# Expert and output projections of part 2: one fp32 product of unsplit operands where three products of fp16 halves stood

## The reference

```python
rw = _gating(hidden_states, sim_matrix, gates)          # (b, t, 16), softmax over the active experts
q = jnp.einsum('bte,bted->btd', rw, jnp.einsum('btc,ecd->bted', hidden_states, q_proj))
k = jnp.einsum('bte,bted->btd', rw, jnp.einsum('btc,ecd->bted', hidden_states, k_proj))
v = jnp.einsum('bte,bted->btd', rw, jnp.einsum('btc,ecd->bted', hidden_states, v_proj))
scores = jnp.einsum('bqd,bkd->bqk', q, k) * scale       # scale = 1/8, causal
attn = jnp.einsum('bqk,bkd->bqd', jax.nn.softmax(scores, axis=-1), v)
mixed = attn[:, :, None, :] * rw[..., None]
return jnp.einsum('bted,edc->btc', mixed, o_proj)
```

## Time and profile before

| what | value |
|---|---|
| median of 3 timed runs | 1654.61 us (1653.49 to 1655.23) |
| profiled execution, from first to last instruction | 1653.4 us |
| PE busy | 1530.0 us (93%) |
| DVE busy | 1406.8 us (85%) |
| ACT busy | 1156.5 us (70%) |
| POOL busy | 1032.0 us (62%) |
| L743 MATMUL (experts) | x1536, 143.8 us busy |
| L783 MATMUL (y) | x768, 48.8 us busy |
| mean granted TensorE clock | 0.977 |

### The profile page before, as it was taken

One profiled execution on the slowest core, in us unless ns is written; L12 is line 12 of the kernel. 1 busy time (PEld: TensorE's weight loads), 2 busy tenths in 40 slices (PEclk: granted clock), 3 DMA queues, 4 the chain that ended last, 5 costly groups with the idle time before them and its releaser, 6 DMA issues. The chain is left out here.

```text
span 1653.4 us, 28187 instructions
## 1 busy us (share of the span) xinstructions
PE 1530.0 (93%) x8882; PEld 844.4 (51%) x8882; DVE 1406.8 (85%) x2161; ACT 1156.5 (70%) x2191; POOL 1032.0 (62%) x715
## 2 busy tenths in 40 slices
PE   3699999999999999999999999999983599999997
PEld 1344444444434444444444444444432599998997
DVE  5999999989999999999999899999997466656665
ACT  3888887788878877777788787787763355545553
POOL 3777777777777777777777677777773433323330
PEclk8999999999999999999999999999996799999999
DMA  4221111111211111111111111111002000000000
GB/s 110 68 62 44 43 27 44 27 46 37 54 26 43 30 38 43 26 43 37 51 32 43 26 43 43 26 26 26 1 1 52 1 6 8 8 9 8 7 9 10
DMA packets 51462, 53.00 MB, mean 32 GB/s; under 512 B 17057, under 2 KB 32929, under 8 KB 51361
## 3 DMA queue, kind: packets, MB, share of 16 engines
q1 hardware_dynamic: 51360, 51.76, 12.3%
HBM read 7.68 MB, written 2.10 MB: 6 GB/s over the span
## 5 line engine op out<-in xcount | busy, mean ns | idle before, releaser
L472 POOL TENSOR_TENSOR prob<-prob 128x1024 f32<-128x1024 f32 x256 | 603.7, 2358 | 252.1 <-DVE prob L1264 251.9
L911 ACT ACTIVATE prob<-score_ps,negmax 128x1024 f32<-128x1024 f32 x512 | 571.2, 1116 | 170.0 <-DVE negmax L1223 158.5
L1223 DVE TENSOR_REDUCE negmax<-score_ps 128x1 f32<-128x1024 f32 x512 | 620.1, 1211 | 64.2 <-PE score_ps L576 62.8
L605 PE MATMUL attn_ps<-probT,v_sb 128*64 128x512 f32 x1024 | 536.2, 618 | 0.8 <-ACT attnT L928 0.8
L576 PE MATMUL score_ps<-ka,qa 128*128 128x512 f16 x1024 | 311.8, 387 | 34.3 <-ACT prob L911 22.8
L840 ACT ACTIVATE probT<-trans_ps 128x512 f32<-128x512 f32 x480 | 285.4, 595 | 6.9 <-PE trans_ps L599 6.9
L599 PE MATMUL trans_ps<-ident,prob 128*128 128x128 f32 x2048 | 269.6, 274 | 2.5 <-POOL prob L472 2.5
L599 PEld LDWEIGHTS trans_ps<-ident,prob 128*128 128x128 f32 x2048 | 240.0, 141 | 56.4 <-POOL prob L472 3.9
L524 POOL TENSOR_TENSOR xs<-xnT,rw_all 128x2048 f32 (+1 forms) x32 | 115.5, 3611 | 210.1 <-PE t_ps L729 203.4
L576 PEld LDWEIGHTS score_ps<-ka,qa 128*128 128x128 f16 x1024 | 69.6, 98 | 341.1 <-ACT prob L911 274.4
L468 POOL TENSOR_TENSOR prob<-prob,ccol 128x384 f32<-128x384 f32 x256 | 211.6, 827 | 49.9 <-DVE ccol L1236 31.1
(11 more groups left out here) (196 smaller groups left out, 1425.4 us busy)
## 6 DMA issues: line engine op xcount, KB each, us to landing
qa<-split SPq DMA_DIRECT2D x256, 64.0 KB, 2.0
ka<-split SPq DMA_DIRECT2D x256, 64.0 KB, 2.0
xg<-xnT SPq DMA_DIRECT2D x16, 512.0 KB, 3.0
resid<-in_L_attn_x SPq DMA_DIRECT2D x4, 512.0 KB, 5.9
wg<-in_L_attn_Wkv SPq DMA_DIRECT2D x32, 64.0 KB, 1.9
out<-yo SPq DMA_DIRECT2D x32, 64.0 KB, 1.5
wg<-in_L_attn_Wq SPq DMA_DIRECT2D x16, 64.0 KB, 1.9
ew<-in_L_ffn_q_proj SPq DMA_DIRECT2D x1, 512.0 KB, 4.4
```

The lines of the kernel that those rows point to most:

```text
L472: pool.tensor_tensor(prob1[:, u, :], prob1[:, u, :], prob2[:, u, :], ALU.add).then_inc(mix_ok, 1)
L605: return pe.matmul(attn_ps[head * DV:(head + 1) * DV, :], v_sb[:, (half // 2) % 2, kt, head * DV:(head + 1) * DV], probT[:, half % 2, kt, ...
L911: act.activation(prob2[:, s % 4, :] if sub else prob1[:, s % 4, :], score_ps[:, sub, :], ACT.Exp, bias=negmax[:, s % 2, sub:sub + 1], accu ...
L1223: dve.tensor_reduce(negmax[:, s % 2, sub:sub + 1], score_ps[:, sub, :], AX.X, ALU.max, negate=True).then_inc(max_ok, 1)
```

## The change

The operands of both projections stay fp32 and are not split. `experts` issues one fp32 product for each expert (16 a tile, 128x128 by 128x192), y one for each pair of experts (8 a tile). The fp16 halves of the weights, their scale of 64, and with them four ACT passes and two POOL passes before part 2, are gone. Each bank of `t_ps` is now read once, as fp32, bank 0 by ACT and bank 1 by DVE, in place of ACT and then DVE for each bank. So a bank's next use, and the product that reads the group, wait for one engine (`xT_A` or `xT_V`, `mT_A` or `mT_V`) where they waited for the second of two.

```diff
--- before.py
+++ after.py
@@ -509,10 +506,6 @@
...
             pool.wait_ge(resid_ok, 2 * STEPS)
-
-            for n, (w, split_w) in enumerate(((ew, ew_split), (eow, eow_split))):
-                pool.wait_ge(w_hi, n + 1)
-                pool.tensor_tensor(split_w[:, 1, :, :], w[:, :, :], split_w[:, 0, :, :], ALU.subtract).then_inc(w_lo, 1)
             pool.wait_ge(g_nP, 2)
@@ -691,7 +684,7 @@
...
             gate_logits(B - 1)
-            pe.wait_ge(w_lo, 2)
+            pe.wait_ge(experts_in, 16 * 5)
             pe.wait_ge(rw_ok, 1)
@@ -706,18 +699,18 @@
-                        pT = (pT_A, pT_V)[bank]
+                        xT, pT, mT = ((xT_A, pT_A, mT_A), (xT_V, pT_V, mT_V))[bank]
                         for what in before:
                             if what == "x0" and live(0):
-                                return pe.wait_ge(xT_lo, 4 * m + bank + 1)
+                                return pe.wait_ge(xT, 2 * m + 1)
                             if what == "x1" and live(0):
-                                return pe.wait_ge(xT_lo, 4 * m + 2 + bank + 1)
+                                return pe.wait_ge(xT, 2 * m + 2)
                             if what == "x1 of m - 1" and live(1):
-                                return pe.wait_ge(xT_lo, 4 * (m - 1) + 2 + bank + 1)
+                                return pe.wait_ge(xT, 2 * m)
                             if what == "p" and live(2):
...
                             if what == "y of m - 1" and live(4):
-                                return pe.wait_ge(mT_lo, 2 * (m - 4) + bank + 1)
+                                return pe.wait_ge(mT, m - 3)
@@ -733,15 +726,13 @@
...
                             return
-                        pe.wait_ge(xT_lo, 4 * m + group + 1)
+                        pe.wait_ge((xT_A, xT_V)[group % 2], 2 * m + group // 2 + 1)
                         if group == 0 and not (first and t == 0):
...
                         for e in range(4 * group, 4 * group + 4):
-                            for n, (x_part, w_part) in enumerate(SPLIT_PRODUCTS):
-                                mm = pe.matmul(qkv_ps[:, 0:3 * DE], xsT[:, t % 2, x_part, e, :], ew_split[:, w_part, e, :],
-                                               start=e == 0 and n == 0, stop=e == E - 1 and n == 2)
+                            mm = pe.matmul(qkv_ps[:, 0:3 * DE], xsT[:, t % 2, e, :], ew[:, e, :], start=e == 0, stop=e == E - 1)
                         if group == 3:
@@ -775,13 +766,12 @@
...
                     if live(4):
-                        pe.wait_ge(mT_lo, 2 * (m - 3))
+                        pe.wait_ge(mT_A, m - 3)
+                        pe.wait_ge(mT_V, m - 3)
                         if not (first and t == 4):
...
                         for g in range(8):
-                            for n, (x_part, w_part) in enumerate(SPLIT_PRODUCTS):
-                                mm = pe.matmul(y_ps[:, 0:C], mxT[:, x_part, g, :], eow_split[:, w_part, g, :],
-                                               start=g == 0 and n == 0, stop=g == 7 and n == 2)
+                            mm = pe.matmul(y_ps[:, 0:C], mxT[:, g, :], eow[:, g, :], start=g == 0, stop=g == 7)
                         mm.then_inc(y_ok, 1)
@@ -972,12 +962,6 @@
-            act.wait_ge(experts_in, 16 * 5)
-            for w in (ew, eow):
-                act.activation(w[:, :, :], w[:, :, :], ACT.Copy, scale=WSCALE).then_inc(w_scaled, 1)
-            for n, (w, split_w) in enumerate(((ew, ew_split), (eow, eow_split))):
-                act.wait_ge(w_scaled, n + 1)
-                act.activation(split_w[:, 0, :, :], w[:, :, :], ACT.Copy).then_inc(w_hi, 1)
             act.wait_ge(g_v, GEXP)
@@ -994,11 +978,10 @@
...
                             act.wait_ge(qkv_ok, m - 1)
-                        act.activation(xsT[:, t % 2, 0, 4 * group:4 * group + 4, :],
-                                       t_ps[:, group % 2, :].rearrange("p (e q) -> p e q", e=4), ACT.Copy).then_inc(xT_hi, 1)
+                        act.activation(xsT[:, t % 2, 4 * group:4 * group + 4, :],
+                                       t_ps[:, 0, :].rearrange("p (e q) -> p e q", e=4), ACT.Copy).then_inc(xT_A, 1)
                     x_copy(0)
-                    x_copy(1)
                     if live(1):
@@ -1026,12 +1008,10 @@
...
                     if live(3):
-                        for bank in range(2):
-                            act.wait_ge(mT_ps, 2 * (m - 3) + bank + 1)
-                            if bank == 0 and not (first and t == 3):
-                                act.wait_ge(y_ok, m - 3)
-                            act.activation(mxT[:, 0, 4 * bank:4 * bank + 4, :],
-                                           t_ps[:, bank, :].rearrange("p (g q) -> p g q", g=4), ACT.Copy).then_inc(mT_hi, 1)
+                        act.wait_ge(mT_ps, 2 * (m - 3) + 1)
+                        if not (first and t == 3):
+                            act.wait_ge(y_ok, m - 3)
+                        act.activation(mxT[:, 0:4, :], t_ps[:, 0, :].rearrange("p (g q) -> p g q", g=4), ACT.Copy).then_inc(mT_A, 1)
                     if live(0):
@@ -1379,19 +1359,19 @@
...
                             return
-                        dve.wait_ge(xT_hi, 4 * m + group + 1)
-                        dve.tensor_tensor(xsT[:, t % 2, 1, 4 * group:4 * group + 4, :],
-                                          t_ps[:, group % 2, :].rearrange("p (e q) -> p e q", e=4),
-                                          xsT[:, t % 2, 0, 4 * group:4 * group + 4, :], ALU.subtract).then_inc(xT_lo, 1)
-
-                    x_copy(0)
+                        dve.wait_ge(xT_ps, 4 * m + group + 1)
+                        if group == 1 and not (first and t < 2):
+                            dve.wait_ge(qkv_ok, m - 1)
+                        dve.tensor_copy(xsT[:, t % 2, 4 * group:4 * group + 4, :],
+                                        t_ps[:, 1, :].rearrange("p (e q) -> p e q", e=4)).then_inc(xT_V, 1)
@@ -1422,19 +1401,18 @@
...
                     if live(3):
-                        for bank in range(2):
-                            dve.wait_ge(mT_hi, 2 * (m - 3) + bank + 1)
-                            dve.tensor_tensor(mxT[:, 1, 4 * bank:4 * bank + 4, :],
-                                              t_ps[:, bank, :].rearrange("p (g q) -> p g q", g=4),
-                                              mxT[:, 0, 4 * bank:4 * bank + 4, :], ALU.subtract).then_inc(mT_lo, 1)
+                        dve.wait_ge(mT_ps, 2 * (m - 2))
+                        if not (first and t == 3):
+                            dve.wait_ge(y_ok, m - 3)
+                        dve.tensor_copy(mxT[:, 4:8, :], t_ps[:, 1, :].rearrange("p (g q) -> p g q", g=4)).then_inc(mT_V, 1)
```

More of the change, by code:

```diff
@@ L87 @@
 GATE_LEAST = 1e-12
-WSCALE = 64.0
 PART2_LAG = 4
@@ L230, in block_kernel @@
         xs = sb("xs", [P, 2, E, C])
-        ew_split = sb("ew_split", [P, 2, E, 3 * DE], F16)
-        eow_split = sb("eow_split", [P, 2, E // 2, C], F16)
-        xsT = sb("xsT", [P, 2, 2, E, P], F16)
+        xsT = sb("xsT", [P, 2, E, P])
         kv2 = sb("kv2", [P, NT, 2 * DE])
@@ L243, in block_kernel @@
         mx = sb("mx", [P, 2, E, DE])
-        mxT = sb("mxT", [P, 2, E // 2, P], F16)
+        mxT = sb("mxT", [P, E // 2, P])
         yo = sb("yo", [P, 2, C])
@@ L274, in block_kernel @@
         const2_in, iota_ok, mask_ok = sem("const2_in"), sem("iota_ok"), sem("mask_ok")
-        g_top, w_scaled, w_hi, w_lo = sem("g_top"), sem("w_scaled"), sem("w_hi"), sem("w_lo")
+        g_top = sem("g_top")
         c2_v, c2_a, c2_p = sem("c2_v"), sem("c2_a"), sem("c2_p")
@@ L279, in block_kernel @@
                                     "normed_V", "T", "A", "V", "lg", "v", "exp", "rw"))
-        (xs_ok, xT_ps, xT_hi, xT_lo, qkv_ok, hi2, lo2, kv_read, kv_first_ok, qkt_ps, qkt_ok, s2_ok, max2, exp2, pT_ps,
-         pT_A, pT_V, pv2, rec2_ok, mx_ok, mT_ps, mT_hi, mT_lo, y_ok, y_done) = (sem("p2_" + n) for n in (
-            "xs", "xT_ps", "xT_hi", "xT_lo", "qkv", "hi", "lo", "kv_read", "kv_first", "qkt_ps", "qkt", "s", "max", "exp",
-            "pT_ps", "pT_A", "pT_V", "pv", "rec", "mx", "mT_ps", "mT_hi", "mT_lo", "y", "y_done"))
+        (xs_ok, xT_ps, xT_A, xT_V, qkv_ok, hi2, lo2, kv_read, kv_first_ok, qkt_ps, qkt_ok, s2_ok, max2, exp2, pT_ps,
+         pT_A, pT_V, pv2, rec2_ok, mx_ok, mT_ps, mT_A, mT_V, y_ok, y_done) = (sem("p2_" + n) for n in (
+            "xs", "xT_ps", "xT_A", "xT_V", "qkv", "hi", "lo", "kv_read", "kv_first", "qkt_ps", "qkt", "s", "max", "exp",
+            "pT_ps", "pT_A", "pT_V", "pv", "rec", "mx", "mT_ps", "mT_A", "mT_V", "y", "y_done"))
         stored = [sem("stored0"), sem("stored1")]
@@ L1044, in tiles2 @@
                             act.wait_ge(qkt_ps, m - 1)
-                        act.activation(qs[:, t % 2, 0, 0:DE], qkv_ps[:, 0:DE], ACT.Copy, scale=DE ** -0.5 / WSCALE).then_inc(hi2, 1)
```

(9 more changed lines are left out.)

4 lines of the change are left out of this document (removed).

## The result

| | before | after |
|---|---|---|
| median of the runs | 1654.92 us (1653.49 to 1655.72, 4 runs) | 1687.36 us (1686.29 to 1689.16, 4 runs) |
| ratio, 95% interval | | 1.0199 [1.0185, 1.0214] |
| profiled span | 1653.4 us | 1684.5 us |
| part 2 starts (first transpose of xs) | 1292.8 | 1288.4 |
| length of part 2 | 360.6 | 396.1 |

A forecast was written before the change was run, and what follows sets the result against it. PE was taken to bound part 2: 54.9 - 10.8 - 4.4 - 1.9 - 3.1 = 34.7 us on the span of 1653.4 gives 1688.1, and a median of 1689.3 us; range 1682 to 1703.

The forecast's parts named there:

- The added products: PE in part 2: fp32 products add 40.7 us in the experts and 14.2 in y, plus 54.9 us.
- Both ends of the range (112 and 214 ns): Bounds for a 192-column fp32 record on PE: experts 12.0 us less than before, or 92 more; 163.5 ns was taken.
- The transposes of mx: PE's waits before and inside these transposes in part 2 shrink from 12.4 to 1.6 us, a gain of 10.8.
- First tiles and tail: PE's waits for bank copies shrink where part 2's pipeline is not filled (4.4 us) and in the last turns (1.9).
- the third of the forecast's three places: One of three places in the first tiles where experts wait behind x transposes; together they gain 2.1 us.
- The gate: On the path to rw_all, L1350 and L1351 on DVE run free of POOL's weight splits: 3.1 us less.
- The stall of PE at the turn of part 2's loop: PE's stall at the loop's turn comes from no data and stays, so no gain was counted.
- The rival of the weight loads: Five groups of fp32 products a turn each pay 0.10 us more: 16 us added, 1705; chance 0.07.
- DVE's copies are not held up by POOL: Rival judged: DVE's copies in part 2 wait until POOL's xs ends, 3.8 us a turn, 1811; chance 0.03.
- That the waits stay: Rival: PE's waits move elsewhere, for example to a late ACT; 10.8 us are not gained, 1700; chance 0.07.
- The faster case: Rival: a 192-column fp32 record costs 112 ns like one of 128, so the kernel takes 1637; chance 0.02.

The follow-up runs named there:

- c64: The changed kernel with 64 columns in place of 192 in the products of the 14 inner experts; 1642.91 us in one run.
- relief_only: The kernel before with each bank read once, three fp16 products kept, xs and mx not split; 1636.46 us, ratio 0.9897.
- work_only: The kernel before with the unsplit fp32 products, each bank still read by ACT and then by DVE; 1704.64 us, ratio 1.0305.
- before_unrolled: The kernel before with PE's loop over batches 1 and 2 in part 2 written out; 1649.05 us, ratio 0.9969.
- after_unrolled: The changed kernel with PE's loop over batches 1 and 2 in part 2 written out; 1687.39 us, ratio to before 1.0197.
- p_first: The changed kernel with the transposes of the probabilities ahead of experts(0); 1686.04 us in one run.

## Why the prediction was right, and where it was not

**The added products** (forecast 54.9). 1024 x 0.1625 = 166.4 for 126.7, and 512 x 0.1117 = 57.2 for 43.0: 39.7 + 14.2 = 53.9. Taking the record's time as twice its columns at 2.4 GHz, from the 512-column row, was right; 163.5 was 1.0 ns too much, for the reason that c64 shows. Both ends of the range (112 and 214 ns) were far off, and the choice between them carried the forecast.

**The transposes of mx** (forecast -10.8). 12.3 us became 1.3: -11.0. relief_only and work_only show that the handover does it and the products do not. (One time on the way was summed wrongly: DVE's copy of bank 1 ends 1.08 + 0.69 = 1.77 us behind the start of the x transposes, not 1.83, and 1.76 in after.)

**First tiles and tail** (forecast -4.4 and -1.9). From x transposes to experts 3.2 became 1.0; the third of the forecast's three places, where experts(2) follows the values product, went from 0.9 to 0.2; from q and k to experts(0) 1.4 became 0.2: -4.2. The three last turns went from 5.6 to 3.6: -2.0, with waits of 1.31, 1.31 and 0.99 (forecast 1.4, 1.4 and 1.0).

**The gate** (forecast -3.1). -3.1 by its rows, and part 2 starts 4.4 us sooner. The other 1.3 are part 1, which the change leaves alone and which varies: in the profiles here part 2 starts anywhere from 1288.4 to 1294.6.

**The step that failed**: "The stall of PE at the turn of part 2's loop comes from no data and stays." It comes from no data, that was read rightly, but code is also something that a change changes. It went: 3.0 us, and 1.5 at the lower clock behind it, -4.5 in all. before_unrolled (part 2 is 4.6 us shorter) and after_unrolled (0) show that these were the loop's.

**The step that was missing**: 3.5 us inside the experts' groups, at the two places where an fp32 record follows a 16-bit product of 56 ns. The rival of the weight loads named the likely mechanism, with 0.10 us at five places a turn; it is 0.056 at two. Its 0.10 came from a row that c64's reading does not explain, since it lies behind a record of 512 columns. p_first shows one of the two places by an edit; the other is read from its row alone (1487.64 to 1489.00, 1.36 us for eight).

Together in part 2: 53.9 - 11.0 - 4.2 - 2.0 - 4.5 + 3.5 = 35.7, measured 35.5; less the 4.4 of the earlier start 31.1, which is the difference of the spans, where 34.7 were forecast. Of the 3.6 too much, 1.0 are the failed and the missing step (opposite in sign, -4.5 and +3.5), 1.3 part 1, 1.0 the record's price, and a few tenths lie in the small terms. The medians differ by 32.4, since after's median lies 2.9 above its profiled span and before's 1.5. That the failed and the missing step nearly cancel was luck, and the time came closer than the steps deserved.

**The other rivals.** DVE's copies are not held up by POOL: the 96 of part 2 have means of 687 and 682 ns, against the 675 and 691 of the earlier trace rows, though POOL's xs runs beside many of them. The groups over the whole kernel:

```profile
L1365 DVE COPY xsT<-t_ps 128x512 f32<-128x512 f32 x64 | 44.0, 687 | 55.0 <-PE t_ps L722 54.8
L1407 DVE COPY mxT<-t_ps 128x512 f32<-128x512 f32 x32 | 21.8, 682 | 0.6 <-PE t_ps L762 0.6
```

The lock of the shared port pair, which the Trainium skill tells of (SBUF — State Buffer, section SBUF: two separate sides), does not show on a copy out of PSUM here, while L1350 and L1351 of the gate did run 1.22 and 1.86 us longer beside POOL's splits; without POOL's splits these two take 0.19 and 0.69. The trace agrees with the rule for those two, whose inputs lie in SBUF; the copies, by their times, are none of the instructions that it is about, as the forecast took them. That the waits stay is refuted by 0.2 us of idle time before L762. The faster case needed a record under 130 ns, and 0.1625 was measured.

## What to carry to other kernels

Read the price of an operation that the trace does not have at the size you need from two neighbouring sizes, and ask whether the smaller one already sits on a floor. Split a change that mixes more work with fewer waits into its two halves: here the handover (one reader for each bank) was worth 17.8 us, and the fp32 products cost 50.4 with the shorter gate and the lost stall already taken off. A stall put down to "issue" at a loop's turn can belong to the length of the loop's code, as here: count the instruction packets in one pass, before and in the changed kernel, and try the loop written out.

## What the runs showed of the hardware

- An fp32 product with a stationary operand of 128 x 128 is two records of twice the columns at 2.4 GHz plus 2.5 ns (0.1625 us at 192, 0.43 at 512), but in a row of short ones no start follows the last by less than about 0.112 us: 64 and 128 columns cost the same (c64, and y in after). So three fp16 products (0.2475 us) beat one fp32 product (0.325) at 192 columns, and at 128 too (0.168 against 0.223).
- These 0.112 us run beside the record ahead. A 64-column fp32 record right behind one of 192 columns takes 0.056 us (c64), and a 192-column one pays 0.056 us extra behind a short record, be it a 16-bit product (after) or a 64-column fp32 one (c64).
- A loop whose body loads code anew in each pass (eight packets of 16 KB) cost PE 3.0 us at the jump and 1.5 us at the lower clock behind it. The same packets cost nothing where the code runs straight on. With 740 records of PE in a pass nothing was loaded again, with 868 and 932 it was.
